# A later clearing on GpSimd, rows turned during the solve, and a shared expert with four iterations open

## What is computed

```python
x = x + _L0_attn_ref(_layernorm(x), ...)   # q, k, v: projection, 4-tap convolution, silu; delta rule; gate
x = x + _L0_ffn_ref(_layernorm(x), ...)    # 8 experts of 176, 2 per token, and a shared expert of 704
x = x + _L1_attn_ref(_layernorm(x), ...)   # 16 heads of 128, causal softmax
x = x + _L1_ffn_ref(_layernorm(x), ...)    # 16 experts of 176, 6 per token
```

```python
def step(S, inp):
    qt, kt, vt, bt = inp
    u = vt - jnp.einsum('bhk,bhkv->bhv', kt, S)
    S = S + bt[:, :, None, None] * kt[..., :, None] * u[..., None, :]
    o = jnp.einsum('bhk,bhkv->bhv', qt, S)
    return (S, o)
```

## Time and profile before

| | us |
|---|---|
| median of three runs | 872.78 |
| lowest, highest | 871.08, 877.59 |
| the profiled execution, its own time | 879.81 |
| its span, first to last instruction | 878.0 |

### The profile page before, as it was taken

The page is one execution under the profiler, slowest core; times in us unless marked ns, Lnnn a source line. Parts: engine busy times, 40 slices in busy tenths (PEclk is TensorE's granted clock), DMA queues, the critical chain, the costliest instruction groups (busy, mean ns, idle before and its releaser), DMA issues.

```text
span 878.0 us, 12769 instructions
## 1 busy us (share of the span) xinstructions
PE 816.9 (93%) x4543; PEld 570.0 (65%) x4543; DVE 462.0 (53%) x1054; ACT 322.8 (37%) x662; POOL 170.3 (19%) x259
## 2 busy tenths in 40 slices
PE   5978789989989995899999999998999999999998
PEld 3456556666657784577777776776766655555557
DVE  5789867666622223775564566557534252232223
ACT  3886767645223313343323234323222211111111
POOL 3656264311610042011111111111100000000000
PEclk9899899999999997999999999999999999999999
DMA  4000294064253321012110101010124344444331
GB/s 138 1 2 1 47 340 144 2 165 137 81 167 108 91 76 45 13 57 76 43 36 25 37 27 34 25 37 25 42 78 128 109 130 128 133 143 126 128 112 48
DMA packets 63957, 72.07 MB, mean 82 GB/s; under 512 B 14200, under 2 KB 48504, under 8 KB 63896
## 3 DMA queue, kind: packets, MB, share of 16 engines
q1 hardware_dynamic: 59048, 64.06, 24.3%
q0 software_dynamic: 1536, 4.20, 1.5%
q10 hardware_dynamic: 3312, 3.02, 1.0%
HBM read 55.45 MB, written 14.75 MB: 80 GB/s over the span
## 4 chain that ended last, share of the span: by engine, by line
PE 80%; DVE 8%; ACT 5%; issue 3%; another core or an unknown queue 1%; SPq 1%; DMA 1%; POOL 1%; DVEq 0%; ACTq 0%; POOLq 0%
PE bank L922 11%; PE bank L880 10%; PE bank L898 10%; PE bank L1096 8%; PE bank L1063 7%; PE bank L961 6%; PE bank L947 6%; PE bank L629 3%; PE bank L1829 3%; PE bank L651 2%; PE bank L1813 2%; PE bank L971 1%; PE bank L1628 1%; DVE sh L2357 1%
## 5 line engine op out<-in xcount | busy, mean ns | idle before, releaser
L922 PE MATMUL bank<-arena 128*128 128x256 f32 x448 | 108.5, 383 | 11.5 <-DVE arena L1231 11.3
L1125 ACT ACTIVATE arena<-bank 128x512 f32<-128x512 f32 (+1 forms) x64 | 34.6, 543 | 230.1 <-PE bank L880 207.0
L922 PEld LDWEIGHTS bank<-arena 128*128 128x128 f32 x448 | 85.1, 191 | 42.2 <-issue 19.6
L1233 DVE TENSOR_TENSOR arena<-arena,bank 128x512 f32<-128x512 f32 (+1 forms) x47 | 30.7, 653 | 151.8 <-PE bank L898 151.8
L880 PE MATMUL bank<-xnT,arena 128*128 128x512 f32 (+1 forms) x256 | 107.9, 544 | 0.0
L898 PE MATMUL bank<-xnT,arena 128*128 128x512 f32 (+1 forms) x256 | 107.1, 541 | 0.0
L1194 ACT ACTIVATE arena<-bank 128x512 f32<-128x512 f32 (+1 forms) x96 | 46.8, 524 | 135.5 <-PE bank L1063 135.5
L848 POOL TENSOR_TENSOR arena<-arena,causal_t 128x256 f32<-128x256 f32 x64 | 45.1, 725 | 258.7 <-ACT arena L1199 258.7
L898 PEld LDWEIGHTS bank<-xnT,arena 128*128 128x128 f32 x256 | 49.2, 192 | 47.8 <-issue 45.9
L1096 PEld LDWEIGHTS bank<-arena 128*128 128x128 f32 x640 | 76.3, 191 | 4.4 <-POOL arena L848 2.9
L1096 PE MATMUL bank<-arena 128*128 128x129 f32 x640 | 77.0, 275 | 1.9 <-POOL arena L848 1.9
(11 more groups left out here) (237 smaller groups left out, 1199.8 us busy)
## 6 DMA issues: line engine op xcount, KB each, us to landing
arena<-in_w_gu SPq DMA_DIRECT2D x60, 256.0 KB, 3.6
rows_in<-place SPq DMA_DIRECT2D x5, 1664.0 KB, 14.1
arena<-in_w_dn SPq DMA_DIRECT2D x56, 128.0 KB, 3.5
arena<-in_wq SPq DMA_DIRECT2D x32, 128.0 KB, 2.1
arena<-in_wo SPq DMA_DIRECT2D x32, 128.0 KB, 2.1
arena<-cw_rows SPq DMA_DIRECT2D x15, 256.0 KB, 3.6
arena<-rows_in SPq DMA_DIRECT2D x23, 128.0 KB, 2.1
rows_out<-arena ACTq DMA_DIRECT2D x23, 128.0 KB, 1.7
```

Source lines behind the costliest of these rows:

```text
L922: mm = nc.tensor.matmul(Y[s][half][l // 2][:, (l % 2) * DIM:(l % 2 + 1) * DIM], hh[:, M % 3, j * P:(j + 1) * P], w_dn[:, slot_of(M), :], s ...
L1125: nc.scalar.activation(sg[:, M % 2, 0:n], ring(M)[0][:, 0:n], ACT.Silu).then_inc(s_silu, 1)
```

## The change

Five edits. POOL clears `place` first and clears `xyf` only after all eight products of the first norm (`ln_xn`). DVE does `cmps(5)` ahead of the weights, ACT makes beta ahead of the second `silu_v` and copies wul ahead of the square root. PE turns solved rows in groups between the sums and the gates, which use bank 0 and 1 now, and ACT copies them in the same order, with the copies of q ahead of all. In the shared expert behind the blocks, gate and up of an iteration share one bank, four such banks go round (`PAIRS`), and down runs `LEAD` = 3 iterations behind; silu waits for up, not for gate.

```diff
     def ring(M):
+        if M < F0B:
+            return (bank[4], bank[5]) if M % 2 == 0 else (bank[0], bank[1])
         if M < F1:
-            return (bank[4], bank[5]) if M % 2 == (0 if M < F0B else F0B % 2) else (bank[0], bank[1])
+            both = bank[PAIRS[(M - F0B) % 4]]
+            return both[:, 0:256], both[:, 256:512]
...
             elif M == F0B:
-                pe.wait_ge(s_silu, F0B)
+                self.done(pe, F0B - 1)
+            elif M == F0B + 1:
                 pe.wait_ge(s_bm, NB - 1)
-            elif M == F0B + 1:
+            elif M == F0B + 2:
                 pe.wait_ge(s_bm, NB)
+            elif M == F0B + 3:
+                pe.wait_ge(s_bye, NB)
+            elif F0B < M < F1:
+                self.done(pe, M - 4)
...
             for M in range(F0B + 1, F0END):
                 self.gate_up(pe, M, attn0)
-                self.down(pe, M - 1, attn0)
-                if M == F0END - 3:
+                if M - LEAD >= F0B:
+                    self.down(pe, M - LEAD, attn0)
+                if M == F0END - 2:
                     self.ln_turn(pe, 4)
-            self.ln_turn(pe, 5)
-            self.down(pe, F0END - 1, attn0)
+            for M in range(F0END - LEAD, F0END):
+                if M == F0END - 1:
+                    self.ln_turn(pe, 5)
+                self.down(pe, M, attn0)
...
         def silu(self, act, M):
-            act.wait_ge(s_pg, M + 1)
+            if F0B <= M < F1:
+                act.wait_ge(s_pu, M + 1)
+            else:
+                act.wait_ge(s_pg, M + 1)
...
             pe.wait_ge(s_kqe, 8)
-            sums(sq[1], s_sqq, bank[6], s_ssq)
...
+            turn_ft(0)
+            sums(sq[1], s_sqq, bank[6], s_ssq)
+            turn_ft(1)
+            turn_ft(2)
+            gates(0)
+            gates(1)
+            turn_ft(3)
+            gates(2)
+            turn_ft(4)
+            gates(3)
+            for i in range(5, 8):
+                turn_ft(i)
...
             kb(7)
-            silu_v(1)
             act.wait_ge(s_b, 2)
             nc.scalar.activation(beta[:], bank[0][:, 0:P], ACT.Sigmoid).then_inc(s_bs, 1)
+            silu_v(1)
...
+            act.wait_ge(s_wt, 1)
+            nc.scalar.copy(wul[:], bank[3][:, 0:P]).then_inc(s_wul, 1)
             act.wait_ge(s_w, 3)
             nc.scalar.activation(kn[:], rkn[:], ACT.Sqrt).then_inc(s_srk, 1)
-            act.wait_ge(s_wt, 1)
-            nc.scalar.copy(wul[:], bank[3][:, 0:P]).then_inc(s_wul, 1)
...
+            for i in range(3):
+                ft_out(i)
+            gates(0)
+            gates(1)
+            ft_out(3)
+            gates(2)
+            ft_out(4)
+            gates(3)
+            for i in range(5, 8):
+                ft_out(i)
...
         def pool(self, pool):
             for t in range(3):
                 pool.memset(pad[t][:, :, :, 0:CONV - 1], 0.0).then_inc(s_pz, 1)
+            pool.memset(place[:], 0.0).then_inc(s_pz, 1)
+            pool.wait_ge(g["ln_xn"], 8)
             pool.memset(xyf, 0.0).then_inc(s_sz, 1)
-            pool.memset(place[:], 0.0).then_inc(s_pz, 1)
...
             taps(11)
+            cmps(5)
             dve.wait_ge(s_ssk, 1)
...
             dve.wait_ge(s_w, 5)
-            cmps(5)
             dve.wait_ge(s_siq, 2)
```

More of the change, by code:

```diff
@@ L890, in up @@
                 pe.wait_ge(s_th, 3 * NH)
-            elif M == F0B:
-                self.done(pe, F0B - 1)
-            elif M == F0B + 1:
-                pe.wait_ge(s_bye, NB)
-            elif M >= 2:
+            elif M >= 2 and not F0B <= M < F1:
                 self.done(pe, M - 2)
@@ L1744, in pe, with gates @@
             pe.wait_ge(s_kqe, 8)
-            sums(sq[1], s_sqq, bank[6], s_ssq)
-            for i in range(4):
+            def gates(i):
+                if i == 0:
+                    pe.wait_ge(s_siv, KD + 4)
                 if i >= 2:
@@ L1774, in units @@
                         pe.wait_ge(s_fta, 8)
+                        pe.wait_ge(s_ge, 4)
                     if i >= 4 and i % 4 == 0:
@@ L1960, in act, with gates, ft_out @@
                 nc.scalar.copy(kq[:, u, :], bank[6 + u % 2][:]).then_inc(s_kqe, 1)
-            for i in range(4):
+            def gates(i):
                 act.wait_ge(s_g, i + 1)
-                nc.scalar.activation(gate[:, 2 * i:2 * i + 2, :].rearrange("p n c -> p (n c)"), bank[4 + i % 2][:],
+                nc.scalar.activation(gate[:, 2 * i:2 * i + 2, :].rearrange("p n c -> p (n c)"), bank[i % 2][:],
                                      ACT.Sigmoid).then_inc(s_ge, 1)
+            def ft_out(i):
+                y, r0, n = i % 2, i // 2 * 4, 2 if i == 7 else 4
+                act.wait_ge(s_ft, i + 1)
+                nc.scalar.copy(ftc[:, :, y, r0:r0 + n].rearrange("p u r -> p r u"),
+                               b_ft[i % 3][:, 0:n * P].rearrange("p (r u) -> p r u", r=n)).then_inc(s_fta, 1)
             for a in range(KD):
@@ L1970, in act @@
             act.wait_ge(s_qc, 1)
-            for i in range(8):
-                y, r0, n = i % 2, i // 2 * 4, 2 if i == 7 else 4
-                act.wait_ge(s_ft, i + 1)
-                nc.scalar.copy(ftc[:, :, y, r0:r0 + n].rearrange("p u r -> p r u"),
-                               b_ft[i % 3][:, 0:n * P].rearrange("p (r u) -> p r u", r=n)).then_inc(s_fta, 1)
+            for i in range(3):
[8 more added lines that the diff above has]
+                ft_out(i)
             def spread(i):
```

10 lines of the change are left out of this document (5 added, 5 removed).

## The result

The changed kernel takes 865.84 us (median of six runs, 863.96 to 867.66), the kernel before 872.12 us (six runs, 871.08 to 877.59). The ratio is 0.9922 with a 95% interval of 0.9897 to 0.9948: 6.8 us faster, 4.5 to 9.0. Forecast were 866.5 us and 6.5 us of gain.

A forecast was written before the change was run, and what follows sets the result against it. PE bounds the kernel from about 340 us; gains come from waits freed on the path at four earlier places. 1.7 + 1.4 + 2.2 + 1.2 = 6.5 us off 872.78 is 866.3, stated 866.5, range 863.5 to 869.5.

The forecast's parts named there:

- the stall: Shared expert: PE idles 8.87 us from 331.46 us; ACT's awaited release comes when POOL's gather issues end; idle stays about as long.
- the fourth term: Shared expert: the end of its tail comes sooner, 1.2 us gained, bounds 0 to 2.
- Clearing behind the norm: First term, at the start: first four norm products take 1.38 instead of 3.06 us; 1.7 us gained, bounds 0.8 and 1.7.
- The rival in which the taps are held by the clearing: Start: taps held while POOL clears, or clock rises no earlier; first term about 0.3, fourth nothing; 868.9 us, chance 0.25.
- Copies ahead of the sums: Second term, 57 to 67 us: DVE's idle 1.59 us ahead of wn goes; 1.4 us gained, bounds 0.5 and 1.6.
- ACT's second table load makes wul late: Ahead of the solve: one more 1.28 us load; by the skill's switch cost, 2.8 us longer, the second term's gain goes.
- Turning as rows become final: Third term, 82 to 111 us: first spread at 102.1 instead of 104.39 us; 2.2 us gained, bounds 1.0 and 2.4.
- silu 16 (348.05) waited for its gate: Shared expert's end: with that gate done earlier, silu 16 follows the copy before it 0.54 us earlier.
- 339.85 stays: Shared expert: DVE's product 13, at 339.85 us after waiting 9.44 us, starts no earlier with the change.
- its own signs: Shared expert: wrong if product 13 starts while POOL still issues; PE's idle about as long, next stage 9.5 to 10 us behind.
- the rival: Shared expert: the stall goes, product 13 starts at 330.4 us, 9.4 us gained, 14.7 with the front; 858 us, chance 0.10.

The follow-up runs named there:

- paced_old_shared: The kernel before with the three parts ahead of the recurrence, old shared expert, and POOL's gathers paced by the shared expert's products: 864.88 us, ratio 0.9929 to before.
- paced_again: The same kernel as paced_old_shared, run once more beside the kernel before at 873.20 us: 864.63 us, ratio 0.9915.
- all_but_shared: The kernel before with the three parts ahead of the recurrence and the old shared expert: 875.63 us against 884.96, ratio 0.9889.
- clear_only: The kernel before with only POOL's clearing of 8448 columns moved behind the eight products of the norm: 884.92 us, ratio 0.9984.
- sums_only: The kernel before with only the copies ahead of the sums, beta ahead of the second silu and wul ahead of the square root: 884.07 us, ratio 0.9986.
- after_again: The whole change, unaltered, run and profiled again on a chip with the stall: 877.57 us against 884.96 for the kernel before, ratio 0.9902.
- before_again: The kernel before, unaltered, run and profiled again on a chip with the stall: 884.96 us, span 881.6 us.
- turns_only: The kernel before with only the turns of solved rows, the gates and the copies of q moved: 879.78 us, ratio 0.9954.
- shared_only: The kernel before with only the new shared expert (banks shared by gate and up, four iterations in flight): 886.56 us, ratio 1.0008.

## Why the prediction was right, and where it was not

The time and the direction were right, and three of the four terms name waits that did go. The picture of the stall was wrong, and the fourth term with it. That 866.5 was met within 0.7 us is in part luck: the 1.2 us of the fourth term did not come, and the three others brought more than their 5.3 us (6.2, 7.4 and 9.8 us in paced_old_shared, paced_again and all_but_shared). The forecast's own sum gives 866.3, and its bounds of 2.3 to 7.7 us give 865.1 to 870.5 rather than the stated 863.5 to 869.5; 865.84 lies in both.

**Clearing behind the norm: 1.7 us forecast.** The products take 1.38 us, the projections start 1.48 us earlier, and the solve ends 1.2 us earlier in clear_only. By its runs it is 1.4 us, 3.5 us faster to 0.7 us slower, so that the gain is shown by the rows of the start and not by the time. The rival in which the taps are held by the clearing is refuted: six taps of 0.76 us. The Trainium skill (GPSIMD Engine Reference, 1. Specifications) has contention with GpSimd for DVE instructions with two SBUF inputs. The runs agree for GpSimd operations that read two tensors (3.97 instead of 0.75 us) and disagree for its memset.

**Copies ahead of the sums: 1.4 us forecast.** wn came as the working said, without idle time, and the copies at 60.73 against 64.39 us. About 0.9 us is left at the end of the solve in sums_only, and 1.2 us by its runs (3.2 us faster to 0.6 us slower). In the profile after a part of the rest went to PE's clock. From PE's turn of wn to its first kq products it is 8.86 us after (61.79 to 70.65) and 7.19 us before (65.54 to 72.73): 16 transposes take 3.62 us at 62.01 and 1.91 us at 67.23. The stretches of the kernel after and of before:

```profile
58.70:65.50 6.80, 5.76 (x26) 5.33 (x27) 6.11 (x13) 6.71 (x13) 0.00 (x0) 0.50 0.00 0
65.50:68.90 3.40, 3.40 (x33) 3.40 (x31) 2.20 (x7) 2.27 (x10) 0.00 (x0) 0.99 0.00 0
```

```profile
62.50:65.90 3.40, 3.40 (x38) 2.98 (x30) 3.40 (x8) 1.86 (x3) 0.00 (x0) 0.50 0.00 0
65.90:69.00 3.10, 3.10 (x31) 3.10 (x30) 3.00 (x9) 2.25 (x9) 0.00 (x0) 1.00 0.00 0
```

The lower level was granted for 6.8 us after and for 3.4 us before. In after_again it was 3.4 us there, and the first kq products come 2.52 us ahead of those of before_again (70.29, 72.81), where the first two terms gave 3.1 us. I had priced the clock in the first term and in the last twelve transposes, not here. The fear that ACT's second table load makes wul late did not come true: wul is copied at 62.25 us, and from the first load at 56.24 us on ACT is dense (1.28, 0.28, 1.28, 1.06 and 2.16 us). The Trainium skill (ScalarE: Activation LUTs, What ACT_TABLE_LOAD costs) has 2.66 us for a switch; by an estimate from it wul would have been copied at about 65 us: the trace disagrees.

**Turning as rows become final: 2.2 us forecast.** 2.56 us by the two profiles (4.36 less 1.80), the same in turns_only, and 4.1 us measured with 1.9 to 6.1 as its interval. The mechanism is the one named. What I had not counted is that the old order has PE's gates on the path: with 3.4 us more at the lower clock the distance was 5.9 us, and the new order keeps that off the path. Behind it DVE's twelve spreads took 5.09 instead of 5.97 us, since three of them ran where POOL was idle (0.34 instead of 0.56 us) and none lasted as long as the two beside POOL's products in before (0.70 us). In paced_again they took 5.97 us all the same. At the first scatter the whole change is 5.6 us ahead in the profiles (5.2 us in after_again against before_again), where the three terms gave 5.3.

**Shared expert: 1.2 us forecast, 0.7 us slower measured (1.6 us faster to 3.0 us slower).** The step that failed is the working of the tail: "silu 16 (348.05) waited for its gate". That wait exists only behind a stall, because PE is late then with its last pairs. Beside the stall it did go, as forecast: from product 15 to the next stage it is 3.5 us in after_again and 3.0 us in shared_only, where before took 3.9 us. But the shared add waits for a down there too (1.03 and 1.72 us), and from product 13 to the next stage it is 11.9 and 12.0 us instead of 11.1. If the stretch is a little shorter with the new code (36.1 and 35.6 against 36.7), it is because product 13 starts 1.3 and 0.7 us behind POOL's last issue instead of 2.9. Without the stall PE has long done the last gate, the chain of DVE and ACT sets the end, and the shared add's new wait of 1.58 us for a down takes the place of what is gained.

**The stall.** The prediction took it for a part of every execution ("339.85 stays") and gave its going away a chance of 0.10 and a time of 858 us. It had gone in the first profile after, and the time was 865.84 us all the same. By its own signs the prediction is wrong here: product 13 starts 8.7 us before POOL's last issue ends, and PE's idle time is 0.93 us instead of about as long as before. On the chips with the stall these signs held (after_again: 8.47 us, product 13 behind POOL's end), except that the next stage came 11.9 us behind product 13 and not 9.5 to 10. A median of before that is 7.7 us below its profiled execution can hardly hold a stall of 10.6 us. The step that failed there is the one ahead of the sum. The profiled execution was 7.0 us slower than the median, and I wrote that I "take the saved microseconds off both", without asking which row held the 7.0 us. The stall of 10.6 us is the row that fits; the chip of those runs is not known, so this is inferred from 871 and 873 us without the stall and 885 us with it. For the sum it did no harm, since no term but the fourth lay in it; for the rival it did, as the rival took 9.4 us off a median that did not contain them.

## What to carry to other kernels

When a profiled execution is slower than the median of the runs by more than their spread, find the row that holds the difference before pricing any edit near it: compare a second profile, stretch by stretch. A part that fills an engine's idle time gains nothing if the wait there ends with another engine's chain; look for the new wait that the longer lead brings. A turn or a copy that stands behind other work in an engine's order hides what a faster engine ahead of it would gain; free it first. Beside VectorE's operations with two SBUF inputs let GpSimd write, not read.

## What the runs showed of the hardware

- A GpSimd tensor_tensor with two SBUF inputs holds a VectorE scalar_tensor_tensor (128 x 512) until it ends: 3.97 to 4.08 us instead of 0.75. A GpSimd memset beside the same taps costs nothing (0.76 us each), though one beside a tensor_scalar of 128 x 256 did: 3.06 us for four instead of 1.38.
- On two chips (seven profiles) TensorE's releases came up to some 10 us late while GpSimd issued 16 gathers by an index, and engines waited for them, 10 us in all. Plain copies by GpSimd in their place, on one of these chips, removed it (875.46 against 884.96 us). On two other chips four profiles show none, three of them of paced kernels.
- TensorE's granted clock falls to 0.5 for stretches of 3.4 us or more whose place and number differ between executions of one kernel: 27.3 us in all in before, 37.5 in before_again, 17.1 to 44.4 us over all profiles. In clear_only there are two behind the first spread, which the profile of before doesn't have, and from the first spread to the first scatter it takes 123.7 us instead of 119.8. In its stretches:

```profile
111.90:115.40 3.50, 3.50 (x34) 2.12 (x31) 0.74 (x3) 1.54 (x6) 3.50 (x9) 0.51 0.97 315
115.40:118.80 3.40, 1.47 (x25) 1.04 (x27) 3.22 (x6) 2.32 (x8) 2.95 (x6) 0.99 1.08 376
118.80:122.20 3.40, 3.40 (x24) 2.37 (x24) 1.09 (x4) 0.00 (x0) 0.00 (x0) 0.50 1.08 385
```

  The runs follow the clock: of the 35 of the kernel before on chip 13 the two with a mean granted clock of 0.984 took 879.8 us, the four with 0.973 took 887.4 to 889.4. So the times of one kernel differ by more than a part of this change is worth, and 12 runs beside 35 left each part uncertain by 2 us.
